# Turning the attention probabilities by 32x32 blocks on VectorE and by SBUF to SBUF transfers, in place of TensorE transposes

## The reference

```python
xn  = layernorm(x)
q   = rmsnorm(xn @ Wq.T)          # 32 heads of 128
k   = rmsnorm(xn @ Wk.T)          # 8 key/value heads, each shared by G = 4 query heads
v   = xn @ Wv.T
p   = softmax(q @ k.T / sqrt(128) + slope * (kpos - qpos), causal)
s   = (p @ v) @ Wo.T
g   = silu(ffn(xn))               # gate, up (1376 wide), silu(gate) * up, down
out = x + s * g
```

## Time and profile before

| what | us |
|---|---|
| median of 3 runs | 2454.89 (2452.98 to 2455.07) |
| the profiled execution's own time | 2455.46 |
| its span, first to last instruction | 2453.7 |
| PE busy | 2422.6 (99%) |
| DVE busy | 1693.7 (69%) |
| ACT busy | 1236.1 (50%) |
| POOL busy | 756.9 (31%) |
| one unit of attention, 530.75 to 658.78 us | 128.0 |

### The profile page before, as it was taken

One profiled execution on the slowest core, in us unless ns is written; L12 is line 12 of the kernel. 1 busy time (PEld: TensorE's weight loads), 2 busy tenths in 40 slices (PEclk: granted clock), 3 DMA queues, 4 the chain that ended last, 5 costly groups with the idle time before them and its releaser, 6 DMA issues.

```text
span 2453.7 us, 37432 instructions
## 1 busy us (share of the span) xinstructions
PE 2422.6 (99%) x13232; PEld 2070.7 (84%) x13232; DVE 1693.7 (69%) x3788; ACT 1236.1 (50%) x2548; POOL 756.9 (31%) x2053
## 2 busy tenths in 40 slices
PE   7999999999999999999999999999999999999998
PEld 6888888888888888878888888888888888888887
DVE  7777777777778787823377787777777777777132
ACT  4555554555545555543355555555555545545333
POOL 2323231413233323244522232323232314131443
PEclk9999999999999999999999999999999999999999
DMA  3010000000000000023320101010000000010232
GB/s 130 1 40 4 27 18 27 18 27 18 27 18 27 18 27 18 27 91 125 112 78 1 44 1 44 1 44 1 27 18 26 18 27 18 1 44 14 90 103 103
DMA packets 23289, 92.19 MB, mean 38 GB/s; under 512 B 6592, under 2 KB 6720, under 8 KB 19136
## 3 DMA queue, kind: packets, MB, share of 16 engines
q1 hardware_dynamic: 23104, 89.80, 10.5%
HBM read 85.60 MB, written 4.19 MB: 37 GB/s over the span
## 4 chain that ended last, share of the span: by engine, by line
PE 96%; DVE 2%; ACT 1%; issue 1%; POOL 0%; DMA 0%; DVEq 0%; ACTq 0%; POOLq 0%
PE out_ps L401 17%; PE score_ps L377 16%; PE out_ps L414 14%; PE qkv_ps L351 14%; PE ring_ps L388 10%; PE qkv_ps L352 7%; PE score_ps L504 5%; PE qkv_ps L504 4%; PE ring_ps L520 4%; PE ring_ps L359 2%; PE out_ps L520 1%; PE ring_ps L364 1%; PE score_ps L351 0%; DVE y L997 0%; DVE xT_lo L868 0%
## 5 line engine op out<-in xcount | busy, mean ns | idle before, releaser
L597 ACT ACTIVATE pT_hi<-ring_ps 128x512 fp32r<-128x512 f32 x576 | 344.0, 599 | 509.8 <-PE ring_ps L388 497.2
L818 DVE TENSOR_TENSOR pT_lo<-ring_ps,pT_hi 128x512 fp32r<-128x512 f32 x576 | 396.8, 690 | 90.6 <-ACT pT_hi L597 86.0
L589 ACT ACTIVATE probs<-probs,low_min 128x896 f32<-128x896 f32 (+7 forms) x512 | 395.2, 774 | 50.4 <-DVE low_min L810 50.1
L1016 POOL TENSOR_SCALAR rs_x<-sq_sum 128x5 f32<-128x5 f32 x122 | 24.8, 203 | 1128.1 <-DVE sq_sum L749 1128.1
L388 PE MATMUL ring_ps<-ident,probs 128*128 128x128 f32 x2304 | 345.6, 273 | 0.0
L388 PEld LDWEIGHTS ring_ps<-ident,probs 128*128 128x128 f32 x2304 | 281.7, 140 | 42.1
L810 DVE CUSTOM_DVE_ANT_0 probs<-score_ps,rel_sb,slope 128x512 f32<-128x512 f32 (+5 forms) x504 | 301.7, 599 | 5.7 <-PE score_ps L377 4.3
L377 PE MATMUL score_ps<-kv_hi,qT_hi 128*128 128x320 f32 (+4 forms) x760 | 275.6, 363 | 3.0 <-DVE xT_lo L868 2.0
L401 PE MATMUL out_ps<-pT_hi,kv_hi 128*128 128x512 f32 x576 | 265.8, 461 | 2.9 <-DVE pT_lo L818 2.6
L377 PE MATMUL score_ps<-kv_hi,qT_lo 128*128 128x320 f32 (+4 forms) x760 | 261.0, 343 | 0.0
L377 PE MATMUL score_ps<-kv_lo,qT_hi 128*128 128x320 f32 (+4 forms) x760 | 260.3, 342 | 0.0
(11 more groups left out here) (178 smaller groups left out, 5293.5 us busy)
## 6 DMA issues: line engine op xcount, KB each, us to landing
qkv_raw<-w_ffn_dram SPq DMA_DIRECT2D x44, 768.0 KB, 4.2
qkv_raw<-w_qkv_dram SPq DMA_DIRECT2D x15, 1536.0 KB, 6.9
o_raw<-w_o_dram SPq DMA_DIRECT2D x16, 1024.0 KB, 4.8
o_raw<-x_dram SPq DMA_DIRECT2D x4, 1024.0 KB, 6.7
out_dram<-y SPq DMA_DIRECT2D x16, 256.0 KB, 3.7
probs<-x_dram SPq DMA_DIRECT2D x3, 1024.0 KB, 7.9
qkv_raw<-w_qkv_dram SPq DMA_DIRECT2D x4, 384.0 KB, 6.6
probs<-x_dram SPq DMA_DIRECT2D x2, 512.0 KB, 4.8
```

Source lines behind the costliest of these rows:

```text
L589: act.activation(row, row, ACT.Exp, scale=-1.0, bias=low_min[:, i % 2, h, HEAD_CHUNKS[i] - 1:HEAD_CHUNKS[i]], accum_out=row_sum[:, i % 2, ...
L597: act.activation(pT_hi[:, n % SLOTS, :], ring_ps[:, ring_bank(r), :], ACT.Copy).then_inc(ring_high, 1)
L818: dve.tensor_tensor(out=pT_lo[:, n % SLOTS, :], in0=ring_ps[:, ring_bank(r), :], in1=pT_hi[:, n % SLOTS, :].bitcast(F32), op=ALU.subtract) ...
```

## The change

The transposes of the probabilities leave PE. In their place:

- **Layout.** `bias` writes the scores of a tile into `probs` so that the 32 columns of one square of one head lie beside the same square of the other heads (`by_head`); the rows are 4096 columns for both buffers.
- **DVE turns squares** (`turn_blocks`): for each head one DVE transposition of 32x32 squares in place, over the (i+1)*128 columns of the tile. That turns each square, but leaves the squares where they are in the grid.
- **SP moves squares** (`turn_probs` on SP): for each tile sixteen transfers SBUF to SBUF; each takes 32 partitions and puts them at 32 other partitions of `pT_lo`, in runs of 128 float32 (512 bytes), (i+1) runs for each partition. So 16 x 32 x (i+1) runs for tile i, 18,432 in a unit.
- **Lag.** A tile is weighed two tiles behind its scores (LAG = 2 steps) instead of one; its output is projected three steps behind. `pT_lo` has 15 homes of 512 columns, for the blocks of two tiles. `high_probs` and `low_probs` now read the blocks in SBUF; six of the 36 low parts of a unit go to POOL (`POOL_LOWS`).
- **Division late.** The probabilities are not divided. The 4 x 128 reciprocals of a tile go out to DRAM in 4-byte pieces (`rec_away`) and come back spread over all partitions (`rec_home`), and `scale_att` on DVE multiplies the weighed sum by them. Then `high_att` (ACT), and `low_att`, which is now on POOL, and only then `out_project`.
- **Norms.** `square` becomes `squares`: five ACT operations of 128 columns with a sum each; `sum_squares` on DVE is gone.
- **PE order** in a step: `project`, `turn_qk`, `out_project`, all `scores`, all `weigh`. Scores have three PSUM banks in turn instead of two; q, k, v land in two pairs of banks in turn.
- The feed-forward part keeps two slots of high and low gate/up weights instead of three. The last unit of a batch row has eleven steps instead of ten.

The core of the diff:

```diff
+            def turn_probs(U, i):                      # on SP
+                t = tile(U, i)
+                alone(probs_turned, t * G)
+                if t > 2:
+                    alone(weighed, homes_free(U, i))
+                homes = pT_lo[:, HOME_AT[i]:HOME_AT[i] + i + 1, :].bitcast(F32).rearrange("p j (a n) -> p j a n", a=BLOCKS)
+                for a in range(BLOCKS):
+                    for k in range(BLOCKS):
+                        b = (a + k) % BLOCKS
+                        sp.dma_start(homes[b * SQUARE:(b + 1) * SQUARE, :, a], by_chunk[i % 2][a * SQUARE:(a + 1) * SQUARE, 0:i + 1, b]
+                                     ).then_inc(probs_back[t % 2], 16)
...
+            def turn_blocks(U, i, h):                  # on DVE
+                dve.wait_ge(exped, (tile(U, i) - 1) * G + h + 1)
+                row = by_head[i % 2][:, h, 0:(i + 1) * BLOCKS, :]
+                dve.transpose(row, row).then_inc(probs_turned, 1)
...
+            def scale_att(U, i):
+                t = U * TILES + i - LAG
+                dve.wait_ge(weighed, (t - 1) // TILES * TURNS + TURN_AT[(t - 1) % TILES + 1])
+                dve.wait_ge(rec_back[t % 2], ((t - 1) // 2 + 1) * 16)
...
-                for h in range(G):
-                    row = probs[i % 2][:, h, 0:(i + 1) * P]
-                    dve.tensor_scalar(row, row, rec[:, h:h + 1], None, ALU.mult).then_inc(divided, 1)
...
-                    if k < turns:
-                        turn_probs(U, i, k, first)
...
+                for k in range(sooner, chunks):        # on DVE, after add_y
+                    bias(U, i, k)
+                    h, part = divmod(k, HEAD_CHUNKS[i])
+                    if part == HEAD_CHUNKS[i] - 1 and h >= 2:
+                        turn_blocks(U, i, h - 2)
...
+            def low_att(U, i):                         # on POOL
+                pool.wait_ge(att_high, U * TILES + i - LAG)
```

More of the change, by code:

```diff
@@ L317, in store @@
                                      y[:, m, :]).then_inc(stored, 16)
-                feed(load_chunk)
+                units(b, attention)
+                for c in range(2, CHUNKS):
+                    load_chunk(c, c % 2, c // FC)
                 alone(f_d_split, (b + 1) * CHUNKS)
@@ new lines, in step @@
+                if not (last and i >= TILES - 1):
+                    turn_qk(U + (i + 1) // TILES, (i + 1) % TILES, first and i + 1 < TILES)
+                if first and i == 1 and U == 0:
+                    for t in range(HT + 2, TILES):
+                        turn_x(0, t)
+                    pe.wait_ge(xT_low, TILES)
+                chunks = G * HEAD_CHUNKS[i] if i < TILES else 0
+                sooner = 2 if last and i == TILES - 2 else 0
+                for k in range(sooner):
+                    scores(U, i, k, first)
@@ new lines, in step @@
+                    if i == LAG:
+                        high_o(U, 0, not first)
+                        high_o(U, 1, not first)
+                    if i < TILES:
+                        for h in range(G - 1):
+                            exp(U, i, h)
+                        for j in highs[:1]:
+                            high_probs(V, p, j)
+                        highs = highs[1:]
+                        exp(U, i, G - 1)
+                        if i == TILES - 1 and not last:
+                            high_k(U + 1, 0, False)
@@ new lines, in step @@
+                    N, n = U + (i + 1) // TILES, (i + 1) % TILES
+                    if not (last and i >= TILES - 1) and not (first and i == 0):
+                        scale_qk(N, n, first and n)
+                    V, p = U - (i < LAG), (i - LAG) % TILES
+                    lows = [] if i >= TILES + LAG or first and i < LAG else [j for j in range(p + 1) if not on_pool(p, j)]
+                    for j in lows:
+                        if j < HIGH_SLOTS:
+                            low_probs(V, p, j)
@@ new lines, in step @@
+                    lows = [j for j in lows if j >= HIGH_SLOTS]
+                    if first and i == 0:
+                        early_norms(tile(U, 2))
+                    if first and i == 1 and U == 0:
+                        for t in range(HT + 2, TILES):
+                            low_x(0, t)
+                    if not (last and i >= TILES - 1):
+                        low_q(N, n, first and n)
+                        if n:
+                            low_k(N, n, first)
+                    chunks = G * HEAD_CHUNKS[i] if i < TILES else 0
@@ new lines, in step @@
+                    if i == TILES - 1 and not last:
+                        low_k(U + 1, 0, False)
+                    if first and i == 0 and U == 0:
+                        for t in range(HT, HT + 2):
+                            low_x(0, t)
+                    if i < TILES:
+                        for h in (G - 2, G - 1):
+                            for j in lows[:1]:
+                                low_probs(V, p, j)
+                            lows = lows[1:]
+                            turn_blocks(U, i, h)
+                        reciprocals(U, i)
@@ L970, in unit @@
-                    for i in range(TILES + 2 if last else TILES):
+                            dve.wait_ge(rel_in, 16)
+                    for i in range(TILES + LAG + 1 if last else TILES):
                         step(U, i, first, last)
```

710 lines of the change are left out of this document (329 added, 381 removed).

## The result

The changed kernel takes 3439.54 us (median of 4 runs, 3435.16 to 3441.70) against 2454.76 us of the kernel before (2452.98 to 2455.07): ratio 1.401, 95% interval 1.399 to 1.404. It is 40% slower. 2369 us had been forecast, with a range up to 2600.

The account below looks back on a forecast made before the run. PE, busy 99%, was taken to bound the kernel: 2453.7 less 253 for transposes, plus 157 of stalls and 10 at batch-row ends, gave 2368 us of span, forecast 2369 us, 3.5% faster; range 2200 to 2600.

Parts of the forecast that it names:

- The transfers: SP's sixteen transfers a tile: some 8.5 us with waits and reciprocals, under the shortest step, so likeliest they cost nothing.
- The reciprocals have three steps: The reciprocals' way out to DRAM and home: three steps of time, put in at no cost.
- Issue: SP issuing the sixteen transfers: 0.33 to 0.43 us each, 5.3 to 6.9 us a tile.
- The rival that transfers land late: `high_probs` waits for transfers, from 48 ns a run or 0.7 us an issue: about 2520 us, or 2760; 18%.
- PE's share: PE without the probabilities' transposes: 253 us less, a floor of 2201 us, about 111.5 us a unit.
- The ring: Each step's loop from `out_project` through DVE, ACT and POOL back to it: PE stalls 9.8 us a unit, 157 in all.
- Step 2: Third step of a unit: ACT's `high_o` stands ahead of the exponentials and adds 2.5 us to the ring.
- The low parts: DVE's low parts of the probabilities, held by POOL: 0.77 us each on the way through DVE.
- The rival in which DVE and POOL hold each other up: DVE and POOL contend for more than 2.3 us a unit; at 8 us, 2460 us, no change; 9%.
- DVE's turns: 32x32 transpositions on DVE: 1.0 ns a column plus 0.1 us, 21.6 us a unit.
- The two-pass rival: DVE's turns take two passes of 1 ns, 18 us a unit more: 2640 us; 9%.
- named signs of being wrong: Turns of 2 us; long DMA waits of `high_probs` or first `bias`; issues over 0.5 us; low parts averaging 1 us or more.

Follow-up runs that it names:

- k1: The changed kernel with each tile's reciprocals written to DRAM as 512 pieces of 16 bytes, output wrong: 2675.23 us, ratio 1.091.
- g0: The changed kernel, order kept, with reciprocals turned by a 32x32 DVE operation and written to DRAM as 128 rows of 128 bytes: 2612.69 us, ratio 1.064.
- g1: g0 with the two small loads, slopes and norm factors, issued ahead of the sixteen transfers of their steps: 2449.45 us, ratio 0.998.
- k3: The changed kernel, 4-byte pieces kept, with only the two small loads issued ahead of the sixteen transfers of their steps: 3235.88 us, ratio 1.319.
- g2: g1 with four transfers of 128 partitions a tile for sixteen of 32, output wrong: 2449.04 us, ratio 0.998.
- g3: g1 with one transfer for each tile, same bytes in runs of 2 KB and more, output wrong: 2448.38 us, ratio 0.998.
- h1: g1 with `low_att` made on DVE instead of POOL: 2376.41 us, ratio 0.967.
- e3: The changed kernel with `rec_home` issued behind the next tile's sixteen transfers, and reciprocals written to DRAM as 128 rows of 128 bytes: 2828.89 us, ratio 1.153.
- k2: The changed kernel with only the first head's reciprocals written, 128 pieces of 4 bytes, used for all heads, output wrong: 3338.46 us, ratio 1.361.

## Why the prediction was wrong

**The step that failed** is "The transfers", in its sentence "with waits, `rec_away` and `rec_home` some 8.5 us" and the next, "The reciprocals have three steps". They have three steps as seen from `scale_att`. But SP itself waits for their landing, in order, ahead of the next tile's sixteen transfers, and the prediction never named what is queued behind that wait. It also gave the write no price: a layout of 4-byte pieces into DRAM was read as 2 KB and so as nothing. It makes SP wait 9 us. The Trainium skill (DMA: Bandwidth & Descriptors, Specifications and Rules for kernel authors) has two sentences on it that I didn't weigh: under 512 bytes a DMA engine reads, modifies and writes, and a transfer with a strided last dimension takes one descriptor for each element and should be rearranged. For the 4-byte pieces the runs agree that this layout is to be avoided; but pieces of 16 and 128 bytes, under 512 too, landed in 1.8 and 1.6 us, and k1 had as many pieces as the changed kernel, so neither sentence gives the price found here. Against some 8.5 us of SP a tile the runs show 22: 10.7 us of issue for 5.3 to 6.9, and 9 of wait for the reciprocals for at most 3. Taken back one by one from 3439.5 us: pieces of 128 bytes 827 us (g0), the slopes' place 163 (g1). That gives 2449.5, and the whole loss of 985 us against the kernel before is told. In the other order the shares are 204 for the slopes' place (k3) and 786 for the pieces.

**Issue** was priced by the earlier trace rows at 0.33 to 0.43 us and took 0.60. Alone it would have changed nothing, as the rival said (it decided from 0.7 us) and g2 and g3 bear out. The packets of 512 bytes, put at 27 ns, kept a DMA engine 35 ns, under the 48 at which they would have decided. In the order as changed it took half of SP's cycle.

**The slopes** were no term at all. The earlier trace rows show the issue of `inv_slope` itself, and its place behind `turn_probs` and the wait could be read from the order of SP's calls. By g1 and k3 they cost 163 to 204 us.

**The rival that transfers land late** had the sign and the engine that waits (`high_probs` on DMA, 437.8 us), but its mechanism, 48 ns a run or 0.7 us an issue, was not what happened, and its worst time, 2760, lies 680 us under the result. The Trainium skill (DMA: Bandwidth & Descriptors, the anatomy of a DMA), which puts about 2 us of fixed cost on a transfer that GpSimd issues, agrees with the 1.8 to 2.8 us that SP's took to land here. Sixteen of them did overlap, 0.64 us apart.

**PE's share** was right as far as it shows: g1's third step (i = 2, from projection to projection), in which its trace lists no wait of PE, takes 10.4 us where 10.3 was put in for PE. g1 has no transposes in it and, with the waits of SP short and hidden, shows what the forecast was for: 2449.5 us, not 2369. A unit takes 124.1 us (the mean of six, by the starts of the projections), where 111.5 + 9.8 = 121.3 was forecast, 45 us in all. The other 35 are what is left by subtraction, on top of the 10 that had been put in for the ends of the two batch rows. In the program's first 80 us PE waits 4.7, 4.4, 3.2 and 3.4 us, which the sum had at nothing. Nor did it have the clock: the granted clock of g1 is 0.978 in the mean, 0.84 in the first 80 us and 0.93 to 0.94 where the batch rows end and begin (960 to 1100, 1230 to 1290, 2180 to 2300 us). By my estimate from these, up to 33 us of PE's pace are lost there; how much of it the waits would have hidden isn't shown.

**The ring** was the right thing to look for, with an error in three terms. From one start of `out_project` to the next, i = 0 to 7, the prediction comes to 13.7, 14.4, 13.3, 11.9, 14.5, 17.1, 17.5 and 18.3 us (the longer of its two lists and its additions, 120.7). The same steps of g1 take 14.6, 15.6, 13.4, 12.9, 14.2, 17.3, 16.6 and 19.7 us in the mean of twelve units, 124.2 in all. Step 2 is right by luck. Its 2.5 us over the ring's 10.8 were put down to ACT's `high_o`, but what PE waits for at its end, for 2.7 us in front of the next `out_project`, is POOL, with `low_o` of 4.8 us ahead of `low_att`, and the list had POOL's queue only in step 5. In h1 `high_o` still stands where it stood and the step takes 11.2 us, so ACT's part is at most 0.4. The clock behind that pause, 0.9 to 1.6 us in nine of 16 units, was no term; it is what step 3 has too much. The low parts had 0.77 us and took 0.99 (g1), 0.77 only when `low_att` left POOL (h1). The rival in which DVE and POOL hold each other up, at 2460 us, thus comes out nearest to g1, though by more than its own mechanism.

**DVE's turns** had 1.0 ns a column and 0.1 us, and measured 1.03 and 0.17. The two-pass rival is out. The Trainium skill's 311 ns for 128x128 bf16 (VectorE: DVE Perf Modes, The three transpose paths) stands beside 306 ns for 128 columns in fp32 here; my 228 was low.

Of the named signs of being wrong three came: issues over 0.5 us, and long waits of `high_probs` and of the first `bias` on DMA. The third came for another reason than was meant: that `bias` waited for the slopes, not for a tile's squares. Turns of 2 us and low parts of 1 us did not come (0.89 us in the changed kernel).

## What to carry to other kernels

A queue that issues transfers and also waits is an engine like the others: write down its order, and for each wait in it what stands behind. Small transfers that others depend on, here the slopes and the reciprocals' way home, go ahead of a burst of large ones (163 us in g1, 216 between e3 and g0). Count a transfer to DRAM in pieces and look at their size: in a round trip between engines, a turn by 32x32 that makes 4-byte pieces into 128-byte ones took 0.21 us a tile and was worth 827 in all. And where work leaves the engine that bounds, follow the ring that is left through the slow engine's order, not only through its durations.

## What was not expected of the hardware

- Writes to DRAM in pieces of 4 bytes: 128 of them took 8.1 us to land (k2), 512 some 9.6 (from the issue to where SP goes on, in the changed kernel), with the DMA engines idle for all but the first 1.4 to 1.7; 128 of 16 bytes 1.8, 512 of 16 bytes 3.1, 128 of 128 bytes 1.6 (g0). Loads issued behind the 4-byte writes landed late too: `slope` 9.4 us against 1.9 in g0, `qkv_raw` of 1.5 MB 15.0 against 6.6.
- A transfer between two places in SBUF, 32 partitions on each side, took SP 0.60 us to issue whether it moved 16 or 128 KB, where the loads and writes of the same kernel took 0.33 to 0.54 in the median. With 128 partitions it was 0.64 (g2), as one transfer for the whole tile 0.47 (g3).
- A pause of PE of 2.7 us was followed by 3 us of matmuls at half their pace in the unit shown, so that the stall cost 4.1. After equal pauses in six other units the clock stayed full.
- In fp32 a turn by 32x32 blocks took 306 ns for 128 columns, 686 for 512 and 1230 for 1024.
